# Merged attention stage: in the first pair of each later block, turnings and one projection item issued ahead of the scores, queries laid out a pair later

## The reference, cut to what matters

```python
Q = (q @ Wq.T + bq).reshape(bs, sl, H, HD)      # q = layernorm(x), H = 16, HD = 32
K = (k @ Wk.T + bk).reshape(bs, sl, H, HD)      # k = v = ctx_2048
V = (v @ Wv.T + bv).reshape(bs, sl, H, HD)
score = jnp.einsum('bshd,bsgd->bshg', Q, K)
weight = jax.nn.softmax(score, axis=-1)
attn = jnp.einsum('bshg,bsgd->bshd', weight, V).reshape(bs, sl, nf)
x = x + jnp.tanh(g_xattn[1]) * (attn @ Wo.T + bo)
```

## Time and profile before

| | us |
|---|---|
| median of 3 runs | 2006.67 |
| lowest, highest | 2000.9, 2008.91 |
| the profiled execution's own time | 1998.72 |
| its span | 1996.9 |
| PE busy in the span | 1913.5 (96%) |
| DVE, ACT, POOL busy | 998.1, 752.5, 1098.9 |
| merged stage, from its first instruction to the next stage's | 1393.2 to 1681.9 |

### The profile page before, as it was taken

How to read it: one execution, slowest core, us unless ns; L and a number is a source line. 1 busy time by engine, 2 the same in 40 slices (tenths; PEclk the granted TensorE clock), 3 DMA queues, 4 the chain that set the end, 5 groups by cost and what they waited for, 6 DMA issues and landing times. The chain is left out here.

```text
span 1996.9 us, 29500 instructions
## 1 busy us (share of the span) xinstructions
PE 1913.5 (96%) x10300; PEld 1606.3 (80%) x10300; DVE 998.1 (50%) x1670; ACT 752.5 (38%) x1147; POOL 1098.9 (55%) x986
## 2 busy tenths in 40 slices
PE   8999999999999999989999899998999997999998
PEld 6888888988888888967777799998777775778886
DVE  5446444745466444663333333333888876771111
ACT  4327343644336332632121221222444454434333
POOL 6765688549756777454116855640544435833333
PEclk9999999999999999999999999999999997999999
DMA  5231332223322423334136755532898666240000
GB/s 175 85 116 54 117 116 95 75 86 127 105 80 69 148 85 126 115 134 163 40 117 202 245 170 186 155 109 73 250 258 227 180 170 219 87 127 21 21 21 21
DMA packets 172283, 248.10 MB, mean 124 GB/s; under 512 B 44992, under 2 KB 69568, under 8 KB 172160
## 3 DMA queue, kind: packets, MB, share of 16 engines
q1 hardware_dynamic: 157072, 202.09, 32.1%
q0 software_dynamic: 9472, 34.09, 5.1%
q10 hardware_dynamic: 5616, 10.23, 1.3%
HBM read 179.77 MB, written 66.58 MB: 123 GB/s over the span
## 5 line engine op out<-in xcount | busy, mean ns | idle before, releaser
L262 POOL TENSOR_TENSOR a_w_hl<-a_w_raw,a_w_hl 128x512 fp32r<-128x512 f32 x232 | 303.9, 1342 | 140.9 <-ACT a_w_hl L341 140.9
L477 PE MATMUL a_proj<-a_c_hl,a_w_hl 128*128 128x512 f32 x768 | 180.5, 394 | 9.1 <-DVE a_w_hl L597 8.7
L477 PE MATMUL a_proj<-a_w_hl,a_c_hl 128*128 128x512 f32 x768 | 181.2, 392 | 0.0
L551 PE MATMUL a_proj<-a_w_hl,a_a_hl 128*128 128x512 f32 x768 | 178.7, 391 | 0.8 <-DVE a_a_hl L681 0.8
L477 PEld LDWEIGHTS a_proj<-a_c_hl,a_w_hl 128*128 128x128 f32 x768 | 144.1, 189 | 41.5 <-DVE a_w_hl L597 10.9
L477 PE MATMUL a_proj<-a_a_hl,a_w_hl 128*128 128x512 f32 x768 | 176.4, 390 | 0.0
L371 ACT ACTIVATE a_sq<-a_proj,a_vecs 128x512 f32<-128x512 f32 x128 | 88.1, 688 | 212.9 <-PE a_proj L477 143.5
L2642 POOL TENSOR_TENSOR f_a_hl<-f_act_sb,f_a_hl 128x512 fp32r<-128x512 f32 x64 | 86.1, 1347 | 148.9 <-ACT f_a_hl L2690 148.8
L477 PEld LDWEIGHTS a_proj<-a_a_hl,a_w_hl 128*128 128x128 f32 x768 | 143.6, 188 | 29.7
L341 ACT ACTIVATE a_w_hl<-a_w_raw 128x2048 fp32r<-128x2048 f32 x59 | 112.8, 1911 | 144.8 <-PE a_proj L477 106.7
L551 PEld LDWEIGHTS a_proj<-a_w_hl,a_a_hl 128*128 128x128 f32 x768 | 142.9, 188 | 30.2 <-issue 1.2
(11 more groups left out here) (269 smaller groups left out, 3494.5 us busy)
## 6 DMA issues: line engine op xcount, KB each, us to landing
a_w_raw<-in_a_vi_w SPq DMA_DIRECT2D x16, 1024.0 KB, 4.9
a_w_raw<-in_a_q_w SPq DMA_DIRECT2D x16, 1024.0 KB, 4.9
a_w_raw<-in_a_o_w SPq DMA_DIRECT2D x16, 1024.0 KB, 5.3
a_w_raw<-in_a_ki_w SPq DMA_DIRECT2D x15, 1024.0 KB, 5.7
spare<-in_b_gate_up POOLq DMA_DIRECT2D x32, 352.0 KB, 3.3
l_sorted_rows<-b_zeros SPq DMA_DIRECT2D x39, 256.0 KB, 3.7
spare<-l_sorted_rows SPq DMA_DIRECT2D x39, 256.0 KB, 3.2
l_expert_out<-spare ACTq DMA_DIRECT2D x39, 256.0 KB, 3.5
```

The source lines that it names most:

```text
L262: ins = pool.tensor_tensor(w_hl[:, s, 1, k], w_raw[:, s, k], f32(w_hl[:, s, 0, k]), ALU.subtract)
L477: mm = pe.matmul(proj[:, j, :], left, right, start=(k == 0 and n == 0), stop=(k == KC - 1 and n == 2))
L551: mm = pe.matmul(proj[:, j, :], a_hl[:, ap, k, j * P:(j + 1) * P], w_hl[:, i % 2, wp, k], start=(n == 0 and m == 0), stop=(n == 4 * G - 1 ...
```

## The change

Three edits, all in `l1_attention`, which act at p = 8, 16 and 24:

1. PE: `scores(p)` is issued behind the first item and the two `turn` of that pair, ahead of the second item.
2. ACT: `move_queries(b)` is issued at place 0 of block b, behind that pair's part of the first item and its two `copy_turned`, in place of place 7 of the block before, where it stood behind the two `copy_turned` and ahead of `exponents`.
3. DVE: `normalise(p - 1)` is issued ahead of `own_scores(2p)`, not between it and `own_scores(2p + 1)`.

```diff
@@ ACT @@
                 if p < NP * NBLK:
-                    if b + 1 < NBLK and w == 7:
-                        move_queries(b + 1)
+                    if p and w == 0:
+                        move_queries(b)
                     exponents(p)
@@ PE @@
             for p in range(NP * NBLK + LAG):
+                first = 0 < p < NP * NBLK and p % NP == 0
                 if p < NP * NBLK:
-                    scores(p)
+                    if not first:
+                        scores(p)
                     item(BESIDE[2 * p])
                 if TURN_LAG <= p < NP * NBLK + TURN_LAG:
                     turn(2 * (p - TURN_LAG))
                     turn(2 * (p - TURN_LAG) + 1)
+                if first:
+                    scores(p)
                 if p < NP * NBLK:
                     item(BESIDE[2 * p + 1])
@@ DVE @@
+                if p and w == 0:
+                    normalise(p - 1)
                 own_scores(2 * p)
-                if p:
+                if w:
                     normalise(p - 1)
                 own_scores(2 * p + 1)
```

## The result

The changed kernel takes 2014.18 us (median of 10 runs, 2010.53 to 2017.96); the kernel before takes 2006.56 us (median of 10, 2000.9 to 2008.91). The ratio is 1.0043, 95% interval 1.0032 to 1.0053, that is +8.6 us (6.4 to 10.6); the two medians are 7.6 us apart. The forecast was 2013, +7 us. A second series on another occasion gave 1.0042 (1.0028 to 1.0057).

What follows compares the result with a forecast made beforehand. PE was taken to bound the merged stage up to pair 23, then DVE; `scores` waits for ACT's `move_queries`. Terms 1.8 + 3.1 + 2.05 = +7.0 us, added to the median 2006.67, gave 2013 us; range 2004 to 2021.

Steps and rivals of the forecast that it cites:

- the likeliest case: Merged stage: `scores` come late behind ACT's chain, +7 us (bounds +2 to +12), giving 2013 us; chance 0.60.
- ACT's chain decides: Pairs 8, 16, 24: ACT's work now ahead of `move_queries` sets when `scores` starts; 3.1, 5.2 and 2.5 us late.
- The chain's length: ACT from DVE's end of `subtract_max` to `move_queries`: 3.44 us in sum; at pair 24 0.68, 0.6 and 0.97.
- Idle ahead of the three scores: PE stalls left behind the turnings at pairs 8, 16 and 24: 4.5, 4.8 and 3.2 us.
- Pair 8: `scores` 3.1 us late, part of it made up by work already done; +1.8 us, bounds +0.2 and +3.5.
- The clock's term: Pair 8: loss to PE's low clock after the stall, some 1.6 us as before the change.
- Pair 16: Next `scores` +2.2 us, plus 0.9 for `scores` at half clock: +3.1 us, bounds +0.5 and +6; nothing saved afterwards.
- rival D: Milder clock: low stretches begin and end sooner, falling in time lost anyway; +2 us, about 2008.5; chance 0.13.
- Pair 24: `scores` 2.5 us late, next `scores` +1.15, plus 0.9 for half clock: +2.05 us, bounds +1.1 and +3.
- B: Not slower: ACT reaches `move_queries` before PE finishes the moved work; -2.9 us, or -4.5, about 2002; chance 0.07.
- C: Stalls of 3 to 5 us each bring a long low-clock stretch; +12.5 us, about 2019; chance 0.20.
- The rule on transposes: PE transposes don't count as clock activity, so `scores` runs at half clock: +7.0 us; if they did, 5.2.

Runs made afterwards that it cites:

- the second profile at pair 24: The changed kernel, unchanged, profiled and timed again; ratio 1.0042 (1.0028 to 1.0057) against the kernel before.
- the second profile of before: The kernel before, unchanged, profiled and timed again as a control; ratio 1.0000 (0.9988 to 1.0013).
- the run with the copy at the head: Changed kernel with ACT's layout copy at the head of pairs 8, 16 and 24, ahead of high part and two `copy_turned`; 1.0020 against the kernel before.

## Why the prediction was right, point by point

The time, the sign and the range held, for the reason that was given, and the shift stayed at some 0.5% or less, as the likeliest case had it. The steps:

- *ACT's chain decides.* Right, and shown from three sides: with the copy at its old place the loss can't be measured any more (1.0002, 1.0011), nor directly behind `exponents` (1.0006), and with half of the chain in front of it half of the loss is left (1.0020).
- *The chain's length.* 3.44 us forecast, 3.13 measured (1519.81 to 1522.94). The step from the take to the high part, 1.30 in the earlier trace rows, is 0.96 where the item lies ready; in the earlier trace rows that step held a wait. At pair 24 it was 2.24, as summed (0.68 + 0.6 + 0.97).
- *Idle ahead of the three scores.* 4.5, 4.8 and 3.2 us forecast; 4.22, 4.36 and 3.39 measured, 3.08 in the second profile at pair 24.
- *Pair 8.* +1.8 forecast, with the clock's loss unchanged at 1.6 us. Measured +2.5 (13.22 against 10.75). The part without the clock was right: +0.2 forecast, and 10.79 against 10.75 with matmuls in the gap. The clock's term was mis-sized: 2.4 us, by the same run, because the item behind `scores` ran at the half clock for longer (4.54 us, not 3.34).
- *What the forecast leaned on without saying:* that the stall of 2.79 us stands for the kernel. It doesn't. In the second profile of before it was 0.52, and up to `weigh` 12 the change costs 4.8 us against that one.
- *Pair 16.* The next `scores` was to come 3.1 us later; it came 3.5 later (11.78 from `weigh` 12, 8.28 before). "Nothing is saved" from there was wrong: by `scores` 18 it is +2.3, twice (18.13 and 18.19 against 15.81 and 15.78), partly since the clock came back to full sooner (`weigh` of pair 14, the last group ahead of `scores` 18, took 1.07 us and not 1.66), partly since a wait of PE for DVE was gone. The first two rows are of before, the third of after:

```profile
1585.31 1.12 PE L2211 MATMUL p_proj<-p_ident,p_hn 128*128 128x128 f32 x4 [0.56 <-DVE p_a_hl L2329]
1588.92 1.66 PE L2268 MATMUL p_out<-p_probs,p_v 128*32 128x128 f32 x16
1602.29 1.07 PE L2268 MATMUL p_out<-p_probs,p_v 128*32 128x128 f32 x16
```

  The clock's part is rival D's mechanism, in this one place.
- *Pair 24.* +2.05 forecast; +1.3 to +4.5 by the stretches, +2.4 and +3.4 like against like. `scores` was to start 2.5 us later, and did in the second profile (5.18 us behind `weigh` 20, 2.65 before). The 0.9 us for the half clock were put on that `scores`; there they fell on the next one.
- *Sum.* 7.0 forecast, 9.2 by the profiles, 8.6 by the times. Over the two profiles of each kernel, `weigh` 4 to `weigh` 12 is +3.7, `weigh` 12 to `scores` 18 +2.4, `weigh` 20 to `scores` 26 +2.9, the rest +0.3. So the terms at pairs 8 and 24 were low (1.8 and 2.05) and that at pair 16 high (3.1). They cancel in part, and that the sum came so near is partly luck.
- *The rivals.* B's point of decision, ACT at the copy before the queries land, was missed by some 3 us: the copy started 4.7 us behind `weigh` 4 (1518.22 to 1522.94), and in the first profile of before the queries landed 1.85 behind it. C needed +12.5; the bounds of the timed shift end at 10.6.
- *The rule on transposes.* I had given +7.0 with it and +5.2 without. The measured `scores` at the half clock (2.08 us) seemed to speak for the rule, but the run with transposes in the gap speaks against it: the moved turnings, 1.5 us of work, ended 4.2 us ahead of `scores`, and it is that idle time that let the clock fall.

## What to carry to other kernels

To fill a wait with work, look at the engine that ends the wait, not only at the one that waits: here PE's moved turnings were free, but ACT's copies of them came to stand ahead of the very instruction that PE was waiting for. Count every instruction between the last input and the signal, on the signalling engine, in its own order. And before a stall of one profile is made the prize of an edit, see it in a second execution: the stall behind a transfer that was 2.79 us here was 0.52 in the next.

## What the runs showed of the hardware

PE transposes of float32 128x128 blocks held TensorE at 2.4 GHz as matmuls did. With 24 of them (2.84 us) in the gap, the granted clock was 1.00 in the next 4 us and `scores` took 1.16 us at pairs 8 and 16; with 4.22 and 4.36 us of idle time instead, the clock was 0.50 and `scores` took 2.08 us, in both profiles of the changed kernel to 0.01 us. Pair 24 decides nothing on this. The Trainium skill, "TensorE: Matmul & The Clock Gate", Part 4 (PE-mode transpose), has it that such a transpose does not count as activity for the clock in the way that a matmul does; here the measurement decides, for this form.

The length of a stall alone does not tell where the low clock begins: after 3.39 us of idle time `scores` of pair 24 took 1.87 us, after 3.08 us 1.16 (in two profiles), and after 2.11 us, in the run with the copy at the head, 1.88.

A stall can cost more than its length: at pair 8, needless work in the gap made the pair 2.4 us shorter than idle time did, with `scores` starting at the same moment.
